# Fourth layer's attention: key tiles taken two at a time, with the next batch's maxima in groups of five

## The reference, cut to what matters

```python
v = (values @ Wv.T).reshape(N, Lv, HEADS, HEAD_DIM)      # N = 8 batches, Lv = Lk = 1500
k = (keys @ Wk.T).reshape(N, Lk, HEADS, HEAD_DIM)        # HEADS = 16, HEAD_DIM = 8
q = (query @ Wq.T).reshape(N, Lq, HEADS, HEAD_DIM)       # Lq = 56
energy = jnp.einsum('nqhd,nkhd->nhqk', q, k)
attn = jax.nn.softmax(energy / jnp.sqrt(jnp.float32(D)), axis=3)
out = jnp.einsum('nhql,nlhd->nqhd', attn, v).reshape(N, Lq, D)
return out @ Wo.T + bo
```

## Time and profile before

| what | value |
|---|---|
| time, median of 3 runs | 1021.73 us (1020.85, 1021.73, 1029.56) |
| span of the profiled execution, first to last instruction | 1024.6 us |
| time of the profiled execution as a whole | not listed; its span alone is 2.9 us above the median |
| PE busy / DVE / ACT | 797.4 / 660.1 / 411.9 us |
| the fourth layer's attention with its first maxima | 749 to 922 us of the span |
| in it: first maxima of batch 0 | 749.1 to 764 us |
| in it: eight batches | 766.1 to 922 us, 19.4 to 19.9 us each from the second to the seventh |

### The profile page before, as it was taken

The page is one execution under the profiler, slowest core; times in us unless marked ns, Lnnn a source line. Parts: engine busy times, 40 slices in busy tenths (PEclk is TensorE's granted clock), DMA queues, the critical chain, the costliest instruction groups (busy, mean ns, idle before and its releaser), DMA issues.

```text
span 1024.6 us, 16576 instructions
## 1 busy us (share of the span) xinstructions
PE 797.4 (78%) x5460; PEld 576.0 (56%) x5460; DVE 660.1 (64%) x1423; ACT 411.9 (40%) x660; POOL 195.9 (19%) x117
## 2 busy tenths in 40 slices
PE   5289888889744358798589999993379999995897
PEld 4267656567433126665268888882125665653565
DVE  5988999987954664255554454435767887834653
ACT  4257556667410103143244444430105555660431
POOL 3344434534203030035120000001050000000011
PEclk9688888898866566689789999996559999996999
DMA  8444353543232000011502342206603445500220
GB/s 256 153 149 144 132 177 124 159 154 117 108 108 18 1 0 2 1 46 47 133 12 64 77 110 63 63 1 82 130 0 90 108 105 125 151 27 2 74 99 19
DMA packets 56680, 87.84 MB, mean 86 GB/s; under 512 B 16570, under 2 KB 41882, under 8 KB 54378
## 3 DMA queue, kind: packets, MB, share of 16 engines
q1 hardware_dynamic: 56634, 87.23, 30.5%
HBM read 55.56 MB, written 31.65 MB: 85 GB/s over the span
## 4 chain that ended last, share of the span: by engine, by line
PE 49%; DVE 15%; issue 2%; ACT 2%; POOL 2%; DMA 1%; DVEq 0%; POOLq 0%; ACTq 0%
PE ps L932 9%; PE ps L922 6%; PE ps L1008 5%; DVE arena L1439 5%; PE ps L1017 4%; PE ps L996 4%; PE ps L867 2%; PE ps L1082 2%; PE ps L821 2%; PE ps L1092 2%; PE ps L1021 2%; DVE arena L1965 1%; PE ps L880 1%; POOL arena L1370 1%; DVE arena L1454 1%
## 5 line engine op out<-in xcount | busy, mean ns | idle before, releaser
L1439 DVE TENSOR_TENSOR arena<-ps,arena 128x448 f32<-128x448 f32 (+7 forms) x156 | 96.5, 646 | 67.3 <-ACT arena L1311 20.5
L1965 DVE TENSOR_REDUCE arena<-ps 112x1 f32<-112x500 f32 x192 | 116.8, 671 | 23.1 <-PE ps L996 23.0
L1292 ACT ACTIVATE arena<-ps 125x896 f32<-125x896 f32 x96 | 87.2, 917 | 107.9 <-PE ps L1008 107.9
L932 PEld LDWEIGHTS ps<-arena 125*112 125x112 f32 (+1 forms) x832 | 105.0, 178 | 14.1 <-issue 5.3
L932 PE MATMUL ps<-arena 125*112 125x129 f32 (+1 forms) x832 | 111.6, 277 | 0.6 <-ACT arena L1276 0.6
L1370 POOL TENSOR_TENSOR arena<-arena 112x4 f32<-112x4 f32 x13 | 13.3, 1021 | 506.5 <-DVE arena L1459 506.5
L1439 DVE TENSOR_TENSOR arena<-ps,rn 125x448 f32<-125x448 f32 x96 | 60.0, 624 | 71.9 <-PE ps L922 66.5
L639 PE MATMUL ps<-w_k2h,arena 128*125 128x512 f16 x288 | 79.1, 437 | 33.1 <-ACT arena L1131 32.9
L1276 ACT ACTIVATE arena<-arena,kbias 125x448 f32<-125x448 f32 x96 | 63.8, 669 | 76.7 <-PE ps L932 71.7
L922 PE MATMUL ps<-arena 128*125 128x448 f16 (+3 forms) x312 | 79.9, 365 | 3.0 <-DVEq L1450 3.0
L639 PEld LDWEIGHTS ps<-w_k2h,arena 128*125 128x125 f16 x288 | 43.5, 156 | 63.3 <-ACT arena L1131 37.9
(11 more groups left out here) (272 smaller groups left out, 1416.5 us busy)
## 6 DMA issues: line engine op xcount, KB each, us to landing
d_k<-arena SPq DMA_DIRECT2D x24, 375.0 KB
d_v<-arena SPq DMA_DIRECT2D x8, 1125.0 KB
arena<-d_k SPq DMA_DIRECT2D x96, 93.8 KB
arena<-d_v SPq DMA_DIRECT2D x8, 1008.0 KB
d_cln<-arena SPq DMA_DIRECT2D x8, 750.0 KB
d_clnT<-arena SPq DMA_DIRECT2D x8, 750.0 KB
arena<-d_clnT SPq DMA_DIRECT2D x8, 750.0 KB
arena<-in_ctx SPq DMA_DIRECT2D x8, 672.0 KB
```

The source lines that it names most:

```text
L932: mm = pe.matmul(dst, pexp[(t + p) % 2][0:rows, TT * c:TT * c + TT], cln_s[p][0:rows, t, :], start=(t == 0 and c in (0, 3)), stop=(t == KT ...
L1292: act.activation(p3[t % 2].rearrange("p (k h) q -> p k (h q)", k=2), ps[0:KP, 2 * (t % 2):2 * (t % 2) + 2, 0:8 * S], ACT.Exp).then_inc(l3_ ...
L1439: return dve.tensor_tensor(out, a, b, op)
L1965: dve.tensor_reduce(mx3[:, u % 8, u // 8:u // 8 + 1], ps[0:TT, MAX_BANKS[u % 3], 0:500], AX.X, ALU.max)\
```

## The change: what it does

The loop over 12 tiles becomes a loop over 6 pairs. In TensorE's queue each pair issues the `sim3` of the two tiles of the next pair, then five maxima (four for the fifth pair, none for the sixth), then the two `pv3` of its own tiles. The first pair's two `sim3` stand ahead of the loop. The probabilities get four buffers instead of two, with the counts of `l3_pv` raised by two to suit: an exponential now waits for the value product four tiles back. `turn_maxima` stands ahead of the last two `pv3`. No instruction is added or removed on any engine but for the two extra buffers; the three maximum banks, the four similarity banks and all waits but those for `l3_pv` stay.

```diff
-        p3 = [carve([KP, 16, S]) for _ in range(2)]
+        p3 = [carve([KP, 16, S]) for _ in range(4)]
...
-                    sp.wait_ge(l3_pv, KT * (b + 1) + 2)
+                    sp.wait_ge(l3_pv, KT * (b + 1) + 4)
...
-                              p3[t % 2][:, 3 * g:3 * g + 3, :].rearrange("p h q -> p (h q)"),
+                              p3[t % 4][:, 3 * g:3 * g + 3, :].rearrange("p h q -> p (h q)"),
...
-            UNITS = (3, 2, 3, 2, 2, 3, 2, 3, 2, 2, 0, 0)
+            UNITS = (5, 5, 5, 5, 4, 0)
...
                 sim3(b, p, 0)
+                sim3(b, p, 1)
                 u = 0
-                for t in range(KT):
-                    if t + 1 < KT:
-                        sim3(b, p, t + 1)
-                    for _ in range(UNITS[t] if more else 0):
+                for pair in range(KT // 2):
+                    if pair + 1 < KT // 2:
+                        sim3(b, p, 2 * pair + 2)
+                        sim3(b, p, 2 * pair + 3)
+                    for _ in range(UNITS[pair] if more else 0):
                         max_sim(b + 1, 1 - p, u, loads + p)
                         u += 1
-                    if t == 0:
+                    if pair == 0:
                         pe.wait_ge(l3_ldv[p], 32 * loads)
                         pe.wait_ge(l3_o, b + 1)
-                    if more and t == KT - 1:
+                    if more and pair == KT // 2 - 1:
                         turn_maxima(b + 1)
-                    pv3(b, p, t)
+                    pv3(b, p, 2 * pair)
+                    pv3(b, p, 2 * pair + 1)
...
-                        act.activation(p3[t % 2].rearrange("p (k h) q -> p k (h q)", k=2),
+                        act.activation(p3[t % 4].rearrange("p (k h) q -> p k (h q)", k=2),
...
-            dve.nop().then_inc(l3_pv, 2)
+            dve.nop().then_inc(l3_pv, 4)
...
-                dve.wait_ge(l3_pv, KT * (b + 1) + 2)
+                dve.wait_ge(l3_pv, KT * (b + 1) + 4)
```

More of the change, by code:

```diff
@@ L1021, in pv3 @@
                     mm = pe.matmul(ps[32 * g:32 * g + 32, 6, 168:280], v3s[p][:, t, 128 + 32 * g:160 + 32 * g],
-                                   p3[t % 2][:, 12 + 2 * g:14 + 2 * g, :].rearrange("p h q -> p (h q)"),
+                                   p3[t % 4][:, 12 + 2 * g:14 + 2 * g, :].rearrange("p h q -> p (h q)"),
                                    start=False, stop=(t == KT - 1), skip_group_check=True)
                 mm.then_inc(l3_pv, 1)
-            UNITS = (3, 2, 3, 2, 2, 3, 2, 3, 2, 2, 0, 0)
+            UNITS = (5, 5, 5, 5, 4, 0)
             def batch3(b, p, loads, more=True):
```

## The result

The changed kernel takes 1046.57 us in the median of 4 runs (1045.81 to 1047.99), the kernel before 1021.82 us (1020.85 to 1029.56, 4 runs). The ratio is 1.0231, with an interval of 1.0198 to 1.0264: slower by some 24 us. The forecast was 1052 us, in a range of 1042 to 1062. The profiled execution took 1045.81 us, its span is 1044.0 us.

What follows compares the result with a forecast made beforehand. PE's queue of similarities, maxima and value products was taken to bound a batch (19.88 us). Seven batches at +4.48 us less 1.2 in the last gave +30.2, put on the 1021.73 median: 1052 us, range 1042 to 1062.

Steps and rivals of the forecast that it cites:

- the sum of 30.2: Whole stage: +4.48 us a batch in seven batches (+31.4) and -1.2 in the last batch, total +30.2 us.
- The ring holds a burst of five: Maxima, three banks: fourth and fifth wait for reductions, value products start 2.13 us after the first maximum; each burst loses 0.98.
- Nothing covers the first exponentials: Start of a batch: tile 2's similarities wait for the first exponential, first maximum at 2.87 us instead of 0.88; pair 0 6.12.
- The second value product: End of each pair: estimated to add 0.52 us, between 0.43 and 0.60, making 1.12 for both products.
- The two similarity groups: Start of each later pair: 0.85 us for both groups, the second taken as 0.42.
- The tail: End of a batch, through turn and shift: next batch 2.42 us behind pair 4 (before 3.07), 1.53 after the shift row.
- Batch 0: First batch, starting at half the clock: the same +4.48 us as the others, give or take 3 us.
- The last batch: Batch without maxima: pairs bound by PE at 2.07 us each, -1.2 us in all.
- The rival without a hold: Fourth and fifth maxima find banks free: +0.56 us a batch, 1024 us, not slower; chance 0.06.
- The rival of the clock: PE idles and its clock falls to half: 6.5 us a pair, 1100 us if over half the stage; chance 0.05.
- The count of waits: Sign in the profile after: 80 to 90 more waits of maxima for reductions (19 before), about 0.6 and 0.35 us each.
- the prediction's other estimate: Changes between maxima and value products: at 175 ns per saved change, pairs gain some 0.35 us, not 0.2; forecast 7 us lower.

## Why the prediction was right

The mechanism and its parts were as forecast; the sum of 30.2 came out as 24.5, because several terms were set a little high and one far too high. Of the 5.7 us between them 3.1 lie in batches 1 to 6, 2.2 in batch 0 and 0.4 in the last.

- *The ring holds a burst of five.* Shown by three runs: with reductions cut short the hold goes and only in the changed kernel, groups of five alone bring it into the kernel before, and spreading the maxima takes it away. From the first maximum to the value products it was 2.13 by the rows and measured 2.08 (792.50 to 794.58). With the tail behind the last burst it is worth more than the whole loss: with short reductions an inner batch of the changed kernel falls from 23.8 to 19.4 us, 0.4 under the kernel before, though the cover is still missing.
- *Nothing covers the first exponentials.* Shown: tile 2's similarities wait for the first exponential (811.13, 0.61 us), and three maxima put ahead bring the first pair from 6.23 to 4.58, of which 0.6 to 0.8 is the cover and the rest the hold of that burst. The forecast had 6.12 for the pair, with both in it.
- *The second value product* was an estimate of 0.52 between 0.43 and 0.60. Two products together measured 1.08 (794.58 to 795.66), so it adds 0.48. The two similarity groups took 0.81, not 0.85. With the burst this makes the pair 3.97 and not 4.10: 0.4 us a batch over the three inner pairs.
- *The tail.* From the fifth pair's first similarities to the next batch 5.77 us (803.61 to 809.38), where 3.52 + 2.42 = 5.94 was forecast; the next batch came 1.43 after the shift row's start, not 1.53. Together an inner batch lost 3.96, not 4.48.
- *Batch 0* is the single term that was mis-sized most: +2.3 for +4.48, near the edge of what I gave it. The prediction said itself that the hold is shorter at half the clock, and still took the full sum. Its first burst at the lower clock is held for less, and the clock rose somewhat sooner than before (a mean of 0.88 from 759.4 to 784.2 us, against 0.84 from 764.6 to 787.1). How much each of the two is worth no run separates:

```profile
764.42 1.24 PE L996 MATMUL ps<-arena 128*112 128x500 f16 x3
765.90 0.41 PE L996 MATMUL ps<-arena 128*112 128x500 f16 x1 [0.24 <-DVE arena L1968]
766.48 0.41 PE L996 MATMUL ps<-arena 128*112 128x500 f16 x1 [0.17 <-DVE arena L1968]
```

- *The last batch* gained 1.6 instead of 1.2: its pairs took 2.0 us, for 2.07.
- *The rival without a hold* is refuted by the waits. The time it would have given, 1024 us with reductions of full length, can't be had with five in a row and three banks, and stays unmeasured.
- *The rival of the clock* is refuted: 1.00 in every stretch from 774 us to the end of the stage.
- The count of waits I gave (80 to 90 more) was high: the prediction's own bursts make 63, and 62 came on the matmuls. The 0.6 and 0.35 us were delays against an unheld burst, and so they measured 0.52 (1.15 for 0.63) and 0.37 (0.58 for 0.21). The rows of the waits show other figures, 0.35 and 0.17 on the matmuls, 0.80 and 0.46 on the weight loads, because they count from the end of the row before on the same engine.

The pair with short reductions is the nearest to an unheld one, 3.11 us against 3.31, so the saving is 0.20 us a pair, or 0.26 if the 0.06 that its five maxima still lost are taken off. That is what the rows gave, and not the 0.35 of the prediction's other estimate. The Trainium skill, "TensorEngine Tiling (Array Packing)", Key Properties, says that a change of tiling mode drains TensorE. No run here separates such a drain from the rest of what a pair saves.

## What to carry to other kernels

A producer that runs ahead through a ring of n buffers can put n units in a row; each further one in the same place in the queue starts only when the consumer frees a buffer (here one every 0.58 us, where the producer needs 0.21), and everything queued behind it waits too, even when the consumer has idled just before (here for 1.03 us). So when work is grouped, group the part that gains by it and leave the part that feeds a ring spread out: here the value products in pairs with the maxima among the similarities gained 0.9%, where pairs with the maxima in one block lost 2.3%. And whatever stands right behind the first step of a loop is cover for the first latency; see what moves away from there.

## What the runs showed of the hardware that was not expected

Value products of two tiles overlap. The first product's 112-column part uses two of the four strips, and two matmuls of the second product start beside it. The rows don't name strips; that these two run on the free ones is read from the program and not shown:

```profile
794.89 0.27 PE L1021 MATMUL ps<-arena 125*32 125x112 f32 x2
...
794.90 0.34 PE L1017 MATMUL ps<-arena 125*32 125x168 f32 x2
794.99 0.27 PE L1021 MATMUL ps<-arena 125*32 125x112 f32 x2
795.07 0.47 PE L1017 MATMUL ps<-arena 125*32 125x168 f32 x6
```

The second product (line 1017) begins 0.32 us after the first, at 794.90, 0.01 after the first one's narrow part. It adds 0.48 us and not the 0.60 of a product by itself, 0.12 less. That the overlap is what saves this is not shown: the 0.60 also hold the 0.17 us for which the next similarities' weight load waits, and in pairs this wait comes once for two products. Without it a product by itself takes 0.43, less than the 0.48.
